# Between a feed-forward and an attention: norm by pairs of tiles, first queries made in the stacked layout, the others inside the loop

## The reference

```python
x = x + _L0_ffn_ref(_layernorm(x, axis=-1), ...)
x = x + _L1_xattn_ref(_layernorm(x, axis=-1), ctx_2048, mask_BxS2_ik0, ...)
x = x + _L1_ffn_ref(_layernorm(x, axis=-1), ...)

# in _L1_xattn_ref, NH = 16 heads of HD = 16
q = proj(hs, Wq, bq, S)                 # hs @ Wq.T + bq, split into heads
k, v = proj(at, Wk, bk, T), proj(at, Wv, bv, T)
scores = clip(einsum('bhsd,bhtd->bhst', q, k) / sqrt(HD), -50, 50)
probs = softmax(where(attend, scores, -10000.0))
ctx = einsum('bhst,bhtd->bhsd', probs, v)
delta = rs * (ctx @ Wo.T + bo)          # then its own layer norm with gamma and beta
```

## Time and profile before

| | |
|---|---|
| runs, us | 793.4, 795.54, 799.48; median 795.54 |
| profiled execution | 793.57 us, span 791.8 us |
| mean granted PE clock | 0.959 |
| busy in the span | PE 89%, DVE 69%, ACT 50%, POOL 21% |
| first feed-forward | about 201 to 439 us |
| from its last matmul to the first scores | about 439 to 463 us |
| attention loop | about 463 to 683 us |
| second feed-forward and output | about 683 to 792 us |

### The profile page before, as it was taken

One profiled execution on the slowest core, in us unless ns is written; L12 is line 12 of the kernel. 1 busy time (PEld: TensorE's weight loads), 2 busy tenths in 40 slices (PEclk: granted clock), 3 DMA queues, 4 the chain that ended last, 5 costly groups with the idle time before them and its releaser, 6 DMA issues.

```text
span 791.8 us, 14802 instructions
## 1 busy us (share of the span) xinstructions
PE 703.4 (89%) x5471; PEld 532.9 (67%) x5471; DVE 544.1 (69%) x1153; ACT 394.2 (50%) x557; POOL 164.9 (21%) x192
## 2 busy tenths in 40 slices
PE   4899989898778999999999459999999999888990
PEld 3788878798566888888888434445455455567880
DVE  6766566664686666666666637878887888886655
ACT  2633324233412222322322359999999999632540
POOL 5462505330100000000000000000402602641551
PEclk9999999999899999999999869999999999998995
DMA  7356474733604676776778828989868860373545
GB/s 237 127 173 223 139 264 134 258 117 97 227 21 131 218 264 217 232 256 210 239 251 174 141 51 204 166 128 121 177 91 148 139 101 2 102 291 99 163 135 185
DMA packets 57531, 131.67 MB, mean 166 GB/s; under 512 B 12432, under 2 KB 32784, under 8 KB 53888
## 3 DMA queue, kind: packets, MB, share of 16 engines
q1 hardware_dynamic: 54208, 123.46, 58.6%
q0 software_dynamic: 2256, 6.18, 2.2%
q10 hardware_dynamic: 1008, 1.25, 0.5%
HBM read 78.92 MB, written 48.79 MB: 161 GB/s over the span
## 4 chain that ended last, share of the span: by engine, by line
PE 56%; ACT 12%; DVE 11%; issue 10%; DMA 6%; POOL 4%; SPq 2%; POOLq 0%; ACTq 0%; DVEq 0%
PE ps L648 13%; PE ps L649 12%; PE ps L650 12%; ACT p L1294 8%; PE ps L917 5%; PE ps L1092 3%; PE ps L883 3%; DMA raw<-in_ctxN 2%; PE ps L1108 2%; DMA raw<-in_ctxT 2%; POOL cTl L608 1%; POOL cNl L595 1%; ACT cNh L1171 1%; PE ps L659 1%; DMA k_lo<-kl 1%
## 5 line engine op out<-in xcount | busy, mean ns | idle before, releaser
L1294 ACT ACTIVATE p<-ps,kbias 128x1024 f32<-128x1024 f32 (+1 forms) x208 | 210.6, 1187 | 5.5 <-PE ps L883 5.5
L1683 DVE TENSOR_SCALAR p<-p 128x1024 f32<-128x1024 f32 (+1 forms) x208 | 141.3, 690 | 36.9 <-ACT p L1294 35.4
L917 PE MATMUL ps<-p,vsl 128*17 128x256 f32 (+1 forms) x1664 | 116.5, 390 | 1.4 <-DVE p L1683 1.3
L883 PEld LDWEIGHTS ps<-qst,kst 48*128 48x128 f32 (+1 forms) x832 | 60.5, 188 | 67.7 <-ACT p L1294 34.1
L883 PE MATMUL ps<-qst,kst 48*128 48x256 f32 (+1 forms) x832 | 93.5, 325 | 11.8 <-DMA qst<-ql 5.9
L1234 ACT ACTIVATE hh<-h 128x512 fp32r<-128x512 f32 x50 | 31.6, 632 | 137.7 <-DVE h L1615 113.9
L356 POOL TENSOR_SCALAR nv<-mv 128x2 f32<-128x2 f32 x6 | 4.6, 761 | 415.0 <-DVE mv L1715 400.8
L648 PE MATMUL ps<-xTh,w_hi 128*128 128x512 f32 x200 | 80.0, 400 | 5.2 <-DVE h L1611 4.4
L650 PE MATMUL ps<-xTh,w_lo 128*128 128x512 f32 x200 | 79.3, 397 | 0.0
L649 PE MATMUL ps<-xTl,w_hi 128*128 128x512 f32 x200 | 79.3, 396 | 0.0
L917 PEld LDWEIGHTS ps<-p,vsl 128*17 128x17 f32 (+1 forms) x1664 | 36.4, 97 | 41.2 <-DVE p L1683 8.1
(11 more groups left out here) (288 smaller groups left out, 1540.6 us busy)
## 6 DMA issues: line engine op xcount, KB each, us to landing
x_slots<-blank SPq DMA_DIRECT2D x20, 1032.0 KB, 5.9
kst<-k_hi SPq DMA_DIRECT2D x64, 200.2 KB, 7.5
w_raw<-in_w SPq DMA_DIRECT2D x25, 384.0 KB, 3.6
v_one<-vst SPq DMA_DIRECT2D x4, 1768.0 KB, 9.1
vsl<-v_one SPq DMA_DIRECT2D x4, 1768.0 KB, 16.0
kst<-k_lo SPq DMA_DIRECT2D x32, 200.2 KB, 8.3
raw<-in_ctxN SPq DMA_DIRECT2D x12, 512.0 KB, 5.7
k_hi<-kh SPq DMA_DIRECT2D x24, 256.0 KB, 2.6
```

The costliest lines, as they stand in the source:

```text
L883: mm = pe.matmul(ps[0:rows, 2 * (x % RING) + t, c * SEQ:(c + 1) * SEQ], kst[r, job % KSL, c, m * P:m * P + rows], qst[r, b, 2 * g + c, :], ...
L917: mm = pe.matmul(ps[32 * j:32 * j + VW, 6 + job % 2, 0:SEQ], vsl[0:rows, b % 2, at_:at_ + VW], p32[0:rows, x % PBUF, (2 * t + c) * SEQ:(2 ...
L1294: act.activation(p32[0:rows, x % PBUF, :], psf[0:rows, bank * 512:bank * 512 + 1024], ACT.Exp, scale=0.25, bias=kbias[0:rows, col:col + 1] ...
L1683: dve.tensor_scalar(t, t, CLO, CHI, ALU.max, ALU.min).then_inc(p_clip, 1)
```

## The change

The feed-forward's last additions move out of it and are taken by pairs of tiles. Batches 0 and 1 (pairs 0 and 1) are normed first, each pair with means, root and reciprocal of its own. The queries of job 0 (batch 0, g 0) are no longer restacked: the weights of those 4 heads are repeated in `wgh`, `wgl` so that PE's result already has the stacked layout; ACT writes the whole piece into `qst`, DVE replaces the third 16 rows by the low part. The restack of (half 0, g 0) is gone, that of batch 1, g 0 is made the same way. Everything else moves to fixed x in the loop (`early`): query piece 0 at x = 1, piece 1 at 5, batch 1's stacked piece at 9, norms of tiles 4 to 7 at 14 to 17 (their inverse roots by POOL, `inverse_root` twice more), their transposes at 23 and 36, query pieces 2 and 3 at 49 and 61. `q_hi` counts 3, 4, 7, 8 for pieces 0 to 3, `q_lo` 5, 6, 11, 12. The load of the second feed-forward's shared weights (`sh_raw`) moves on SP from ahead of the loop behind `queries(1, 1)`, and their split on DVE from x = 28 to 35 to x = 66 to 73.

```diff
@@ SP
-            for g in range(NG - 1):
+            for g in range(1, NG - 1):
                 queries(0, g)
-            sp.wait_ge(sc_rdy, 1)
-            for k in range(NSH1):
-                sp.dma_start(sh_raw[:, k * WC:(k + 1) * WC], a["w1"][k]).then_inc(d_in[0], 16)
...
             def queries(half, g):
-                n = KT * half + g // 2 + 1
-                sp.wait_ge(q_hi, n)
+                n = KT * half + g // 2
+                sp.wait_ge(q_hi, (3, 4, 7, 8)[n])
                 restack(half, g, 0)
                 restack(half, g, 1)
-                sp.wait_ge(q_lo, n)
+                sp.wait_ge(q_lo, (5, 6, 11, 12)[n])
                 restack(half, g, 2)
...
+                if job == KSL + 2:
+                    sp.wait_ge(ln_T, 8)
+                    for k in range(NSH1):
+                        sp.dma_start(sh_raw[:, k * WC:(k + 1) * WC], a["w1"][k]).then_inc(d_in[0], 16)
@@ POOL
+            pool.wait_ge(ln_mv, 3 * NT)
+            for b in range(2):
+                inverse_root(pool, 2 + b, b)
@@ PE
+            for q in range(2):
+                pair_T(q, q)
+            pe.wait_ge(cw_rdy, 6)
+            pe.wait_ge(ln_lo, 5)
+            for c in range(2):
+                first_queries(0, c, ps[:, 4 + c, 0:SEQ])
+            pe.wait_ge(ln_lo, 6)
+
+            def early(y):
+                if y == 1:
+                    queries(0, 7)
+                elif y == 5:
+                    pe.wait_ge(q_lo, 5)
+                    queries(1, 7)
+                elif y == 9:
+                    pe.wait_ge(q_lo, 6)
+                    for c in range(2):
+                        first_queries(1, c, ps[:, 7, c * SEQ:(c + 1) * SEQ])
+                elif y == 23:
+                    pe.wait_ge(cx_rdy, 1)
+                    pair_T(2, 6)
+                elif y == 36:
+                    pe.wait_ge(cx_rdy, 2)
+                    pair_T(3, 7)
+                elif y == 49:
+                    pe.wait_ge(cx_rdy, 3)
+                    pe.wait_ge(ln_lo, 8)
+                    queries(2, 6)
+                elif y == 61:
+                    pe.wait_ge(cx_rdy, 4)
+                    queries(3, 7)
@@ PE, in qk
-                    if b == 0:
+                    if b == 0 and g == 0:
+                        pe.wait_ge(q_lo, 4)
+                    elif b == 0:
                         pe.wait_ge(q_in[g], 16 * 3 * HG)
+                    elif b == 1 and g == 0:
+                        pe.wait_ge(q_lo, 10)
...
                 if x >= RING:
                     pe.wait_ge(p_exp, x - RING + 1)
+                elif x == 1:
+                    pe.wait_ge(add_rdy, 4)
@@ ACT
+            for q in range(2):
+                act.wait_ge(ln_mv, 2 * NT + 2 * q + 2)
+                act.activation(std[:, 2 * q:2 * q + 2], mv[:, 2 * q:2 * q + 2, 1], ACT.Sqrt, bias=eps[:]).then_inc(ln_std, 1)
+            for q in range(2):
+                pair_hi(q, q)
             act.wait_ge(bq_rdy, 1)
-            for n in range(2 * KT):
...
+            for c in range(2):
+                first_queries_hi(0, c, c + 1, ps[:, 4 + c, 0:SEQ])
+            act.activation(std[:, 4:5], eps[:], ACT.Exp)
...
+            def early(x):
+                if x == 1:
+                    queries_hi(0, 3, 7)
+                elif x == 5:
+                    queries_hi(1, 4, 7)
+                elif x == 9:
+                    for c in range(2):
+                        first_queries_hi(1, c, 6, ps[:, 7, c * SEQ:(c + 1) * SEQ])
+                elif x == 22:
+                    pair_hi(2, 6)
+                elif x == 35:
+                    pair_hi(3, 7)
+                elif x == 48:
+                    queries_hi(2, 7, 6)
+                elif x == 61:
+                    queries_hi(3, 8, 7)
@@ DVE, in the feed-forward's last pair of experts' tiles
+                for w, g in ((wqh, wgh), (wql, wgl)):
+                    for k in range(KT):
+                        heads = w[:, k, 0:HG * HD].rearrange("p (h r) -> p h r", r=HD).unsqueeze(2).broadcast_to([P, HG, 64 // HD, HD])
+                        dve.tensor_copy(g[:, k, :].rearrange("p (h c r) -> p h c r", h=HG, r=HD), heads).then_inc(cw_rdy, 1)
@@ DVE, between the feed-forward and the loop
-            ln_front(1)
-            ln_back(1)
...
+            for q in range(2):
+                tiles_add(q)
+                tiles_mean(q, 1)
+            for q in range(2):
+                dve.wait_ge(ln_std, 4 + q)
+                dve.reciprocal(rstd[:, 2 * q:2 * q + 2], std[:, 2 * q:2 * q + 2]).then_inc(ln_rstd, 1)
+                dve.wait_ge(ln_rstd, 4 + q)
+                tile_norm(2 * q)
+                tile_norm(2 * q + 1)
+            for q in range(2):
+                pair_lo(q, q)
+            tiles_add(2)
+            for c in range(2):
+                first_queries_lo(0, c, c + 1, ps[:, 4 + c, 0:SEQ])
+            tiles_add(3)
+            tiles_mean(2, 2)
```

More of the change, by code:

```diff
@@ L854, in _, with pair_T, first_queries, queries @@
                 return
-            ln_transpose(1)
-            pe.wait_ge(ln_lo, 8)
-            pe.wait_ge(cw_rdy, 2)
-            for n in range(2 * KT):
+            def pair_T(q, bank):
+                pe.wait_ge(ln_xn, 2 * NT + 2 * q + 2)
+                for k in range(KT):
+                    for j in range(2):
+                        mm = pe.transpose(ps[:, bank, (2 * k + j) * P:(2 * k + j + 1) * P], xn[:, 2 * q + j, k * P:(k + 1) * P], ident[:])
+                mm.then_inc(ln_T, 1)
+            def first_queries(b, c, o):
+                s, w = slice(b * SEQ, (b + 1) * SEQ), slice(c * P, (c + 1) * P)
+                for k in range(KT):
+                    mm = mm3(pe, o, wgh[:, k, w], wgl[:, k, w], xTh[:, k, s], xTl[:, k, s], k == 0, k == 1)
+                mm.then_inc(Q_rdy, 1)
+            def queries(n, bank):
                 half, t = n // KT, n % KT
@@ L889, in free_again @@
                 b, r = job // NG - 1, job % NG
+                if job == 1:
+                    pe.wait_ge(q_lo, 10)
+                elif job in (2, 3):
+                    pe.wait_ge(ln_lo, 5 + job)
+                elif job == 4:
+                    pe.wait_ge(q_lo, 11)
                 if 0 < b and r == 1 and b < NB:
@@ L1255, in _, with pair_hi, first_queries_hi, queries_hi @@
                 return
-            ln_std_hi(1)
-            act.wait_ge(bq_rdy, 1)
-            for n in range(2 * KT):
-                half, t = n // KT, n % KT
-                act.wait_ge(Q_rdy, n + 1)
-                act.activation(qh[:, t, half * 512:half * 512 + 512], ps[:, 4 + n, :], ACT.Identity, bias=bq[:, t:t + 1]).then_inc(q_hi, 1)
+            def pair_hi(q, bank):
+                act.wait_ge(ln_T, 4 + q + 1)
+                act.activation(xTh[:, :, q * 256:(q + 1) * 256], ps[:, bank, :].rearrange("p (k n) -> p k n", k=KT), ACT.Copy).then_inc(ln_hi, 1)
+            def first_queries_hi(b, c, number, o):
+                act.wait_ge(Q_rdy, number)
+                act.activation(qst[:, b, c, :], o, ACT.Identity, bias=bq0[:, c:c + 1]).then_inc(q_hi, 1)
+            def queries_hi(n, number, bank):
+                half, t = n // KT, n % KT
+                act.wait_ge(Q_rdy, number)
+                act.activation(qh[:, t, half * 512:half * 512 + 512], ps[:, bank, :], ACT.Identity, bias=bq[:, t:t + 1]).then_inc(q_hi, 1)
+            for q in range(2):
[3 more added lines that the diff above has]
+                pair_hi(q, q)
+            act.wait_ge(bq_rdy, 1)
+            for c in range(2):
[17 more added lines that the diff above has]
+                    queries_hi(3, 8, 7)
             act.wait_ge(kbias_rdy, 1)
@@ L1667, in _, with tiles_add, tiles_mean @@
                 return
-            ln_front(1)
-            ln_back(1)
-            for n in range(2 * KT):
+            def tiles_add(q):
+                x = resid[:, 2 * q:2 * q + 2, :].rearrange("p t d -> p (t d)")
+                dve.wait_ge(down_done, SC0 - 1 + q // 2)
+                dve.tensor_tensor(x, x, ps[:, q, :], ALU.add).then_inc(add_rdy, 1)
+            def tiles_mean(q, n):
+                dve.wait_ge(add_rdy, q + n)
+                for t in range(2 * q, 2 * q + 2 * n):
+                    dve.bn_stats(st6[:, t, :], resid[:, t, :]).then_inc(ln_stat, 1)
+                dve.wait_ge(ln_stat, 2 * NT + 2 * q + 2 * n)
+                for t in range(2 * q, 2 * q + 2 * n):
+                    dve.bn_aggr(mv[:, t, :], st6[:, t, :]).then_inc(ln_mv, 1)
@@ new lines, in tile_norm, with pair_lo, first_queries_lo @@
+            def tile_norm(t):
+                dve.tensor_scalar(xn[:, t, :], resid[:, t, :], mv[:, t, 0:1], rstd[:, t:t + 1], ALU.subtract, ALU.mult).then_inc(ln_xn, 1)
+            def pair_lo(q, bank):
+                dve.wait_ge(ln_hi, 8 + q + 1)
+                s = slice(q * 256, (q + 1) * 256)
+                dve.tensor_tensor(xTl[:, :, s], ps[:, bank, :].rearrange("p (k n) -> p k n", k=KT), xTh[:, :, s].bitcast(F32), ALU.subtract).then_inc(ln_lo, 1)
```

(31 more changed lines are left out.)

43 lines of the change are left out of this document (23 added, 20 removed).

## The result

The changed kernel takes 792.25 us (median of 20 runs, 788.15 to 797.36), the kernel before 794.98 beside it (20 runs, 790.51 to 799.48). The ratio is 0.9963, 95% interval 0.9946 to 0.9980: 2.9 us faster, 1.6 to 4.3. That is within 1%, and inside the range of 779 to 794, but the gain of 8.1 us that the sum gave is not there: a third of it is. Measured a second time on another chip the ratio was 0.9962 (0.9937 to 0.9988), so the 2.9 us are real and so is the shortfall.

A forecast was written before the change was run, and what follows sets the result against it. ACT bounds the loop at 1.0 us per x; ahead of it is a chain with no engine full. 15.7 - 2.6 - 4.3 - 0.3 - 0.4 = 8.1 off 793.57 gives 785.5, 787.4 on the median's scale; forecast 786.5, range 779 to 794.

The forecast's parts named there:

- signs of being right: First exp at 448 to 449.5, exp 10 at 461 to 464, ACT waiting about 4 us at x = 65, unchanged from x = 104.
- The shorter chain: Ahead of the loop: exp 0 at 448.3 or 449.3 against 465.32, 16 to 17 us earlier.
- The table load: Before exp 0: 1.28 us beside DVE's low parts; rival that it costs more than its row, 787.5, chance 0.03.
- The copies in the feed-forward: Last tiles of the feed-forward: four more DVE copies, 1.3 us in all, taken as 0.4, between 0 and 1.3.
- The opening of the loop: Up to exp 10: low clock until x = 1 costs 1.4 us; exp 10 at 462.2, gain 15.7, between 17.1 and 8.9.
- ACT's pieces in the loop: After x = 10: two transposed pairs, two query pieces and a wait at x = 48 cost ACT 2.6 us.
- Stall 4.3: At x = 65: job 5's keys, queued on SP behind a wait for q_hi 7, delay exp 65 by 4.3 us.
- the losses at jobs 6 and 7: Behind the stall, SP catching up on keys and shared weights: 0.3 us put on both.
- the inverse roots: POOL, before the norms at x = 14 and 16: 7.3 us each, costing nothing or a few tenths.
- no stall, the clock holds: Rival at job 5 and the opening: with both, gain 13.8, 780 us; chance of a time below 783: 0.18.
- The low clock stays until x = 10: Rival in the loop's opening: gain 1.3, 792 us, the same if keys are 6 us slower; chance 0.17.
- its own case of 783 to 790: Whole kernel: the forecast's own case, a time of 783 to 790 us, chance 0.56.

The follow-up runs named there:

- all three edits: Changed kernel with job 5's keys issued first, 34 products of zeros on PE, and queries 3's restacks ahead of batch 1's values: 778.65 us, ratio 0.9819 to the kernel before.
- the keys' edit: Changed kernel with SP issuing the second half's query restacks one job later, so job 5's keys go first: 786.80 us, ratio 0.9896 to the kernel before.
- the second trace: Changed kernel run again with no edit, on another chip: 791.83 us, ratio 0.9962 to the kernel before.
- the wait alone in the kernel before: Kernel before with one added SP wait, until exp 49 is done, ahead of the second half's query restacks at job 4: 802.10 us, ratio 1.0094.

## Why the forecast was wrong

Point by point, in the prediction's own steps. Its signs of being right came: the wait at x = 65 with a DMA of `kst` as releaser (5.57 us for about 4), the clock at 1.00 by exp 10, the same length behind x = 104 (108.33 us for 108.08). What was wrong is the size of three terms, the stall's above all.

**The shorter chain: right.** First exp 16.57 us earlier, against 16 to 17. The table load took 1.28 with the next instruction right behind it, so it cost nothing beyond its row. The copies in the feed-forward cost 0.4, as taken: from the feed-forward's first `hh` to its last it takes 220.16 us for 219.80.

**The opening of the loop: 15.7 taken, 14.2 measured,** and 12.8 to 14.2 over five kernels that share it. With the clock held, the gain was 17.3, and 17.1 was the upper bound. So the work was counted rightly and the clock was not: the low stretches cost 3.1 us, not 1.4. The prediction let the clock rise at the first wide queries and stay, and called them the kind of work behind which it had risen fast. In the kernel before it had risen at 450.4 and the first query matmul starts at 451.39, so that reading was wrong. It fell at about 441.4 (0.72 in that stretch), 4.3 us behind the last `down` with eight transposes in between, rose at about 445, fell again at 448.3 among the wide products of x = 1, behind 1.69 us of idling, and rose only at 455.1, in those of x = 5. Reckoned the same way, it had fallen 4.6 us behind the last `down` in the kernel before, with no transposes in between (at 443.6, as 0.80 in the stretch of 443 to 444 says; the prediction read 443.8 and so 4.8, and likewise 450.2 and 477.4 for 450.4 and 477.7). The Trainium skill (TensorE: Matmul & The Clock Gate, Part 4: PE-mode transpose) says of a transpose that it does not count as PE being busy in the way that other matmuls do; by that rule, the transposes should not put off the fall, and the trace agrees (4.3 us with them, 4.6 without). As to the rise, the kernel before still disagrees, as the prediction says: PE had idled for 7.34 us, made 16 transposes from 446.3 to 450.0, and made nothing else before the clock rose at 450.4.

**ACT's pieces in the loop: 2.6 taken, 4.0 measured** (exp 10 to exp 65: 59.29 us with all three edits, 55.27 before). Each of the later ones waits for PE besides: 0.18, 0.78 and 0.31.

**SP's list: the step that failed.** "Stall 4.3" had the right place, cause, releaser and order, but the wrong price: 7.1 us against the keys' edit (6.0 in the second trace), 7.5 by the wait alone in the kernel before. Two things were missing. The wait itself is 5.7 (exp 49 to 65, 23.17 less 17.49). With T for the start of exp 48, `q_hi` 7 came at T + 2.6 for 2.1 and the keys took 3.2 us to issue for 2.2, so they landed at T + 23.2 for 21.7. From there to exp 65 it took 2.4 us with the clock at 0.50, where 1.7 had been taken. Against that, exp 65 would have come at T + 20.0 without the wait, not at T + 19.1. And the sum had no term for what PE does after waiting: it idles 5.18 us, the clock goes to 0.50 for 7 us, and more is lost from exp 65 to 78: 1.1 us against the kernel before, 1.4 against the keys' edit. The prediction had charged an idle PE with the clock in the opening and forgot it in its own stall.

**Not seen: the restacks of queries 3** behind the values of batch 1. Before, ACT reached x = 39 late enough; starting 14 us earlier, it comes to the edge: 0 to 1.6 us in the changed kernel, and all of the gain as soon as the opening is made faster. The prediction counted each thing that SP's list holds back by a wait, and nothing that stands behind a large transfer.

**The sum again:** 14.2 - 4.0 - 5.7 - 1.1 = 3.4 at exp 78 (read: 111.62 - 108.19 = 3.43), less 0.4 for the copies: 3.0. The runs say 2.9. So of the 5.1 us by which 8.1 was too much, the stall and the clock behind it are 2.5, the opening 1.5 and the pieces 1.4, less 0.3 for the losses at jobs 6 and 7 that did not come. Small terms held: nothing for the inverse roots, the same length behind x = 104. Of the rivals, "no stall, the clock holds" with its gain of 13.8 is what the kernel with all three edits became: 14.4. That the numbers lie so near is in part luck, since the pieces cost 1.4 more than that rival has and a third edit was needed. "The low clock stays until x = 10" has 792, the time that was measured, but not the cause: the clock was 1.00 from 455.1 on, 6.7 us before exp 10, and the keys landed 1.5 us late, not 6. (The rivals' times are reckoned from 793.57, some on the scale of 786.5, which is 1 us higher.) Of the prediction's three cases by size, faster by over 1% (0.47), slower by over 1% (0.05) and the rest (0.48), the last came, while its own case of 783 to 790, with 0.56, did not.

## What to carry to other kernels

When work is pulled forward, walk every queue's list from the new start to the end of its look-ahead and ask of each entry both what it waits for and how many bytes are ahead of it: here two lines of SP's list, moved, brought more than three times what the change itself did. Price a stall of the bound engine's feeder at its length plus the clock that it loses behind it, 1.1 to 1.4 us for 5 us of PE idling here. And put a wait that you suspect into the old kernel by itself: one line gave a price of 7.5 us where the changed kernel's traces have 6.0 to 7.1.
